# Expert rows and weights as scaled float16 pairs, the gathered rows transposed by DMA

## The reference

```python
def _sage_layer(h, src, dst, W_self, W_neigh, b, n_nodes):
    agg = segment_sum(h[src], dst, num_segments=n_nodes)
    deg = segment_sum(ones_like(dst), dst, num_segments=n_nodes)
    h_neigh = agg / maximum(deg, 1.0)[:, None]
    return relu(h @ W_self + h_neigh @ W_neigh + b)

x = x + sage(sage(layernorm(x)))
xf = layernorm(x)
topv, topi = top_k(xf @ Wg, 2); gate_w = softmax(topv)
h = relu(einsum('td,edh->teh', xf, W1) + b1)          # 8 experts, 512 x 512 each
y = layernorm(einsum('teh,ehd->ted', h, W2) + b2) * gamma + beta
x = x + sum(gate_w * y at topi)
```

## Time and profile before

| | |
|---|---|
| three runs | 2905.79, 2911.72 and 2912.53 us; median 2911.72 |
| the profiled execution | 2904.27 us, span 2902.5 us |
| mean granted TensorE clock | 0.95 |
| PE, DVE, ACT, POOL busy | 82%, 54%, 29%, 69% of the span |
| layer 1, layer 2, experts | about 140 to 1146, 1175 to 2165, 2192 to 2902 us |

### The profile page before, as it was taken

The page is one execution under the profiler, slowest core; times in us unless marked ns, Lnnn a source line. Parts: engine busy times, 40 slices in busy tenths (PEclk is TensorE's granted clock), DMA queues, the critical chain, the costliest instruction groups (busy, mean ns, idle before and its releaser), DMA issues.

```text
span 2902.5 us, 55359 instructions
## 1 busy us (share of the span) xinstructions
PE 2393.3 (82%) x11308; PEld 1537.2 (53%) x11309; DVE 1566.9 (54%) x3789; ACT 842.7 (29%) x1611; POOL 2004.7 (69%) x2229
## 2 busy tenths in 40 slices
PE   1088887878888777788888888898987999999996
PEld 0044444444444444455555555455556778888885
DVE  8665444545444444344445454444446677777775
ACT  6511211212211111111111111111114555555554
POOL 0277777777777775777777777777755666666665
PEclk9998989998989999899999999999998999999998
DMA  7578999899897776888888788888875765666543
GB/s 272 212 219 301 301 303 306 300 303 301 297 307 244 231 233 187 294 253 260 253 256 258 256 263 254 258 252 259 256 235 135 164 140 119 142 138 133 107 80 62
DMA packets 239323, 663.61 MB, mean 229 GB/s; under 512 B 47224, under 2 KB 48818, under 8 KB 236168
## 3 DMA queue, kind: packets, MB, share of 16 engines
q0 software_dynamic: 151472, 464.79, 55.8%
q10 hardware_dynamic: 62388, 128.09, 12.4%
q1 hardware_dynamic: 25380, 69.89, 7.5%
HBM read 550.93 MB, written 111.69 MB: 228 GB/s over the span
## 4 chain that ended last, share of the span: by engine, by line
POOL 46%; PE 21%; issue 16%; DMA 11%; DVE 2%; ACT 2%; SPq 1%; POOLq 0%; DVEq 0%; ACTq 0%
POOL store_all L728 45%; PE ps L1766 17%; DMA store_all<-h_scratch,srcT 5%; DMA store_all<-xn_scratch,srcT 2%; DMA wts<-expert_weights_scratch 1%; DMA out<-store_all,idx_s 1%; PE ps L1929 1%; PE ps L1941 1%; ACT store_all L857 1%; SPq L394 1%; ACT ln_out L857 1%; DMA xn_scratch<-store_all 0%; DVE ln_bst L1134 0%; PE ps L1796 0%; PE ps L1797 0%
## 5 line engine op out<-in xcount | busy, mean ns | idle before, releaser
L728 POOL DMA_INDIRECT store_all<-xn_scratch,srcT x782 | 776.3, 993 | 356.1 <-issue 230.1
L1796 PE MATMUL ps<-store_all,sel 128*128 x1680 | 682.2, 406 | 331.7 <-SPq L616 274.3
L728 POOL DMA_INDIRECT store_all<-h_scratch,srcT x782 | 760.2, 972 | 256.2 <-issue 224.3
L1797 PE MATMUL ps<-store_all,sel 128*128 x1680 | 671.4, 400 | 0.0
L1796 PEld LDWEIGHTS ps<-store_all,sel 128*128 128x128 f16 x1680 | 172.3, 103 | 698.6 <-issue 642.5
L1766 PE MATMUL ps<-wts,sT 128*128 128x512 f32 x1176 | 446.3, 492 | 0.0
L1766 PE MATMUL ps<-wts,aT 128*128 128x512 f32 x1176 | 400.7, 450 | 0.8 <-DVE aT L1375 0.8
L1337 DVE TENSOR_TENSOR sel<-iota_g,dstT 128x384 f16<-128x384 f32 (+2 forms) x602 | 306.4, 527 | 39.2 <-issue 30.2
L1766 PE MATMUL ps<-wts,m_hT 128*128 (+1 forms) x1224 | 312.9, 404 | 4.2 <-DVE m_hT L1642 4.2
L1766 PE MATMUL ps<-wts,m_xT 128*128 (+1 forms) x1224 | 311.4, 403 | 4.5 <-DVE m_xT L1585 3.6
L1766 PEld LDWEIGHTS ps<-wts,sT 128*128 128x128 f32 x1176 | 239.5, 211 | 93.4 <-issue 39.0
(11 more groups left out here) (299 smaller groups left out, 3063.5 us busy)
## 6 DMA issues: line engine op xcount, KB each, us to landing
expert_weights_scratch<-w_both ACTq DMA_DIRECT2D x64, 512.0 KB
wts<-expert_weights_scratch SPq DMA_DIRECT2D x64, 512.0 KB, 4.9
store_all<-in_L_ffn_W ACTq DMA_DIRECT2D x64, 256.0 KB, 5.5
of_experts<-xn_scratch ACTq DMA_DIRECT2D x49, 256.0 KB
of_experts<-h_scratch ACTq DMA_DIRECT2D x49, 256.0 KB
store_all<-in_x ACTq DMA_DIRECT2D x49, 256.0 KB, 4.8
store_all<-xn_scratch,srcT POOLq DMA_INDIRECT x782, 4.7
store_all<-h_scratch,srcT POOLq DMA_INDIRECT x782, 4.1
```

The lines of the kernel that those rows point to most:

```text
L728: pool.indirect_dma_start(rows[:, t % SLOTS, :], None, rows_d, bass.IndirectOffsetOnAxis(ap=srcT[:, t:t + 1], axis=0)).then_inc(s_rows[t % ...
L1796: pe.matmul(agg_p[p], sel[:, s, :], row[:, 0:D], start=k == 0, stop=False)
L1797: pe.matmul(agg_p[p], sel[:, s, :], row[:, D:2 * D], start=False, stop=False) \
```

## The change

- The experts' weights are multiplied by a power of two, found on the chip, and stored as pairs of float16. Layer 1 reads the weights twice, in 16 chunks of two row blocks: in tiles 4 to 19 DVE takes maximum and minimum of each chunk (`scan`); in tiles 20 to 22 the bounds go through HBM to all partitions and become scales; in tiles 24 to 39 the chunks are split.
- The normed rows are written as float16 pairs scaled by 2^11. Layer 2 has one activation and one subtraction more for it (`norm_lo`), and the store comes after the copy of xT.
- The weights of two experts now fill one half of `wts`, so expert 1 is loaded with expert 0 at the start of layer 2. An expert is four pieces of 512 KB, not eight.
- In the experts ACT issues one DMA transpose per tile, from the gathered pair of rows straight into the transposed operand; PE's four transposes of x, ACT's copy and DVE's subtraction are gone. The products are float16, three passes as before.

The diff, cut to its core:

```diff
+NCH = NB // 2
+SCAN0 = 4
+SPLIT0 = SCAN0 + NCH + 4
+assert SPLIT0 + NCH <= NT - 3
...
 
 
         wts_all = sb("wts", [P, 4, 2, KC, D], F32R)
         wts = [wts_all[:, 2 * i:2 * i + 2] for i in range(2)]
-        wts_e = wts_all[:].rearrange("p a h k n -> p (a h k n)").rearrange(
-            "p (r k h m n) -> p r k h m n", r=2, k=KC, h=2, m=2)
+        wts_e = wts_all[:, 0:2].rearrange("p r h k n -> p r (h k n)").bitcast(F16).rearrange(
+            "p r (c h m b n) -> p r c h m b n", c=2, h=2, m=2, b=2)
         store_all = sb("store_all", [P, 32, D])
         rows, w_raw = store_all[:, 0:SLOTS].bitcast(F16), store_all[:, 24:32].rearrange("p (m k) n -> p m k n", m=2)
-        raw_blocks = store_all[:, SLOTS:SLOTS + 2]
         bias_all = sb("bias", [2, 2, D], F32R)
...
+            loop0 = head
+            for g0, n, more in early:
+                for g in range(loop0, g0):
+                    tile(g, g % 2, between.get(g, {}))
+                pairs(g0, g0 + n, more)
+                loop0 = g0 + n
...
-                for k in range(KC):
+                for c in range(2):
                     for h in range(2):
-                        sp.dma_start(wts_e[:, par, k, h].bitcast(F32), wsplit_d[e * KC + k, :, h] if isinstance(e, int) else
-                                     wsplit_d[bass.ds(e * KC + k, 1), :, h].rearrange("a p m n -> (a p) m n")) \
+                        sp.dma_start(wts_e[:, par, c, h].rearrange("p m b n -> p m (b n)"),
+                                     wsplit_d[e * 2 + c, :, h] if isinstance(e, int) else
+                                     wsplit_d[bass.ds(e * 2 + c, 1), :, h].rearrange("a p m n -> (a p) m n")) \
                             .then_inc(s_expert[par], 16)
                         if landed is not None:
-                            alone(sp, s_expert[par], landed + 16 * (2 * k + h + 1))
+                            alone(sp, s_expert[par], landed + 16 * (2 * c + h + 1))
...
-                    sp.wait_ge(s_wst, 32 * NB + 1)
+                    sp.wait_ge(s_wst, SPLIT_DONE)
                     load_expert(0, 0)
+                    load_expert(1, 1)
...
-            sp.wait_ge(L[1]["dense"], NT)
-            load_expert(1, 1)
...
+            def gather_x(q, half, used=None):
+                if used is not None:
+                    alone(pool, M["xT"][half], used * 16)
...
+                gather_x(q + 3, 1 - half, pair + (1 + half))
...
                 def store_norm(n, p):
-                    alone(act, S["xn2"], n + 1)
+                    alone(act, S["xnlo"], n + 1)
                     if not (isinstance(n, int) and n == 0):
                         alone(act, S["xst"], n * 16)
                     for r in own_rows(n):
-                        act.dma_start(rows_at(xn2_d, n)[r], xn2_t[r]).then_inc(S["xst"], 16)
-
-                def load_raw(b, p):
-
-                    act.wait_ge(s_wset, 2)
-                    alone(act, s_wl, b + 1)
+                        act.dma_start(rows_at(xn2_d, n)[r], pair[r]).then_inc(S["xst"], 16)
+
+                def load_raw(c, p):
+
                     for m, w in enumerate((W1, W2)):
-                        act.dma_start(raw_blocks[:, m], w.rearrange("e (k p) n -> (e k) p n", p=P)[bass.ds(b, 1)]
-                                      .rearrange("a p n -> (a p) n")).then_inc(s_wraw, 16)
-
-                def store_split(b, p):
-                    alone(act, s_wl, b + 2)
-                    for h, t in enumerate((w_hi, w_lo)):
-                        act.dma_start(wsplit_d[bass.ds(b, 1), :, h].rearrange("a p m n -> (a p) m n"),
-                                      t.bitcast(F32)).then_inc(s_wst, 16)
+                        act.dma_start(raw_chunk[p][:, m].rearrange("p (b n) -> p b n", b=2),
+                                      w.rearrange("e (c b p) n -> (e c) p b n", b=2, p=P)[bass.ds(c, 1)]
+                                      .rearrange("a p b n -> (a p) b n")).then_inc(s_wraw, 16)
+
+                def load_scan(c, p):
+                    alone(act, s_scan, c + 1)
+                    load_raw(c, p)
+
+                def load_split(c, p):
+                    act.wait_ge(s_bound, SCANNED + 1)
+                    alone(act, s_wl, c + 1)
+                    load_raw(c, p)
+
+                def store_bounds(c, p):
+                    act.wait_ge(s_bound, SCANNED)
+                    act.dma_start(wmax_d[:, :], w_abs3[:]).then_inc(s_wmove, 16)
+
+                def load_bounds(c, p):
+                    act.wait_ge(s_wmove, 16)
+                    act.dma_start(of_experts[:, 3 * D:3 * D + 3 * P],
+                                  wmax_d.rearrange("(a p) c -> a (p c)", a=1).to_broadcast([P, P * 3])).then_inc(s_wmove, 16)
+
+                def store_split(c, p):
+                    alone(act, s_wl, c + 3)
+                    for h in range(2):
+                        act.dma_start(wsplit_d[bass.ds(c, 1), :, h].rearrange("a p m n -> (a p) m n"),
+                                      w_halves[:, h]).then_inc(s_wst, 16)
...
-                def expert_hi(b, p):
-
-                    alone(act, s_wraw, b * 32 + 32)
-                    act.wait_ge(s_wst, b * 32 + 1)
-                    act.activation(w_hi, raw_blocks, ACT.Copy).then_inc(s_wh, 1)
+                def expert_hi(c, p):
+
+                    alone(act, s_wraw, c * 32 + (NCH + 1) * 32)
+                    act.wait_ge(s_wst, c * 32 + 1)
+                    act.wait_ge(s_bound, SCALED_W)
+                    act.wait_ge(s_wset, 2)
+                    for m in range(2):
+                        i = act.activation(w_halves[:, 0, m], raw_chunk[p][:, m], ACT.Identity, scale=w_sc[:, m:m + 1])
+                    i.then_inc(s_wh, 1)
...
                 def norm2(n, p):
                     act.wait_ge(S["nmr"], n + 1)
                     act.wait_ge(S["xT"], n)
                     act.wait_ge(S["xst"], n * 16)
-                    act.activation(xn2_t, x2_t[:], ACT.Identity, bias=nmr[:, 0:1],
-                                   scale=rstd[:, 0:1]).then_inc(S["xn2"], 1)
+                    for to in (pair[:, 0:D], xn2_t):
+                        i = act.activation(to, x2_t[:], ACT.Identity, bias=nmr[:, 0:1], scale=rstd[:, 0:1])
+                    i.then_inc(S["xn2"], 1)
...
-                    hooks.update({4: [(sqrt2, 2)], 6: [(norm2, 2)], 8: [(store_norm, 2)], 10: [(xT_copy, 2)], 3: [(load_x, 1)]})
-                layer(act, l, hooks, early={4: [load_raw], 11: [expert_hi], 14: [store_split]} if l == 0 else None,
+                    hooks.update({4: [(sqrt2, 2)], 6: [(norm2, 2)], 10: [(xT_copy, 2), (store_norm, 2)], 3: [(load_x, 1)]})
+                layer(act, l, hooks, early=() if l else
+                      ((SCAN0, NCH, {4: [load_scan]}),
+                       (SPLIT0, NCH, {4: [load_split], 11: [expert_hi], 14: [store_split]})),
+                      between={SCAN0 + NCH: {12: [store_bounds]}, SCAN0 + NCH + 1: {12: [load_bounds]}},
                       drain=drain if l else None)
...
-            def x_hi(q):
-                act.wait_ge(M["xT"], q + 1)
-                act.wait_ge(M["h"], q)
-                act.activation(m_xT[:, 0].rearrange("p k n -> p (k n)"), mxT_p, ACT.Copy).then_inc(M["xHi"], 1)
+            def transpose_x(half, landed):
+                alone(act, M["x"][half], landed)
+                act.dma_start_transpose(m_xT[:, half], m_x2[:, half]).then_inc(M["xT"][half], 16)
...
-                    i = act.activation(m_hr[:, k, :], mhT_p[:, k * P:(k + 1) * P], ACT.Relu, bias=bias)
+                    i = act.activation(m_hr[:, k, :], mhT_p[:, k * P:(k + 1) * P], ACT.Relu, bias=bias,
+                                       scale=h_sc[:, 0:1])
...
+            transpose_x(0, 16)
+            transpose_x(1, 16)
+
+            def tile_m(q, half, pair):
...
-                x_hi(q + 1)
...
+                transpose_x(half, pair * 16 + 32)
...
+                def scan(c, p):
+
+                    alone(dve, s_wraw, c * 32 + 32)
+                    for t, op in ((scan_max, ALU.max), (scan_min, ALU.min)):
+                        i = dve.tensor_reduce(out=t[:, bass.ds(c, 1), :].rearrange("p a m -> p (a m)"), in_=raw_chunk[p],
+                                              axis=AX.X, op=op)
+                    i.then_inc(s_scan, 1)
+
+                def own_bounds(c, p):
+
+                    dve.wait_ge(s_scan, NCH + 2)
+                    dve.wait_ge(s_wg, 32)
...
+                def weight_scales(c, p):
+
+                    dve.wait_ge(s_wmove, 32)
+                    bstep(dve.tensor_reduce(out=w_bound[:], in_=w_every.rearrange("p q c -> p c q"), axis=AX.X, op=ALU.max))
...
+
+                def expert_lo(c, p):
+
+                    dve.wait_ge(s_wh, c + 1)
+                    for m in range(2):
+                        i = dve.scalar_tensor_tensor(out=w_halves[:, 1, m], in0=raw_chunk[p][:, m], scalar=w_sc[:, m:m + 1],
```

(57 more changed lines are left out.)

119 lines of the change are left out of this document (80 added, 39 removed).

## The result

The changed kernel takes 2975.28 us (median of 4 runs, 2962.66 to 2985.97) against 2909.02 for the kernel before on the same chip: a ratio of 1.0227 [1.0201, 1.0252]. It is slower, where 2857 us were forecast. The profiled execution is at the upper end of its runs (span 2984.2 us, 81.7 more than before's), so some 15 us of that difference are spread between runs.

A forecast was written before the change was run, and what follows sets the result against it. POOL's gather issue was taken to bound the graph layers and PE the expert stage. From the profiled 2904.3 us, minus 55 (expert tiles) plus 5 (layer 1), 1 (layer 2) and 2 (first tiles) gave 2857 us, range 2810 to 2970.

The forecast's parts named there:

- Layer 1: Tiles that scan or split weights: longer work on DVE and ACT, at most 48 us uncovered, taken as 5 us.
- the cover: Layer 1: PE's own slack, 93.1 us of waits for arrivals in 32 tiles, 2.9 us each, hides the added work.
- Layer 2: Extra activation and subtraction of 0.8 us a tile, covered by ACT's 5.6 us wait for PE; 1 us for the drain.
- The expert tile: Expert stage: period falls from 6.63 to 6.08 us, 0.55 saved in each of 100 tiles, 55 us.
- No idle gap stands on PE, so PE sets this pace: Expert stage before the change: PE's transposes and products fill the 6.63 us tile; 0.1 us off is 10 us off the kernel.
- The DMA transpose: Expert tile: 0.9 us issue on ACT with 2.16 free, 4.9 us landing with 7.7 free, so no cost.
- the scatter chain: Expert stage rival: scatters waiting on one another, 6.58 us apart beside the transpose's 256 KB; 2907 us, chance 0.11.
- Transposes that land late: Expert stage rival: at 8.8 us landing 2912 us, each 2 us more costing another 100; chance 0.05.
- the expert weights' loads: Expert stage: loads halve to four pieces per expert and delayed nothing with PE busy throughout; 0 us.
- The rival that forecast 2972: Expert stage, ACT queue: a transpose issue of 3.31 us makes ACT pace tiles at 7.23 us; chance 0.19.
- The rule that spoke against the change: Expert tile: transpose 128x128 on TensorE, 390 ns against 1309 by DMA; eight blocks 10.5 us, 7.5 us a tile, 2996 us.
- The first tiles: Start of the expert stage: first three tiles gain a transpose's latency in place of PE, ACT and DVE steps; 2 us.

The follow-up runs named there:

- h's chain short: Scale moved off the relu, high half of h first in the second product: changed kernel 2977.5 us; with float32 x transposed on TensorE 2883.7 us.

## Why the prediction was wrong

**Layer 1: right, and cheaper still.** Twelve profiled kernels share after's scan and split tiles: their layer 1 lasts 1007.9 to 1022.6 us, 1013.7 on average, against 1013.3 before. The 5 us forecast were nothing; the cover held, and the 6 us of the profiled execution are spread between runs.

**Layer 2: the wrong cover.** 1 us was forecast, 14 to 18 came. The step named ACT's wait for PE as what hides one more activation and one more subtraction. But its own first paragraph says that the layer lasts as long as POOL's gathers take to issue, and whether the subtraction slows those was not asked. It does, by 13.7 us / 49 = 0.28 us a tile. The Trainium skill has this in "GPSIMD Engine Reference", section Specifications: POOL's way to SBUF is shared with VectorE, and VectorE instructions with two SBUF inputs contend with it. The subtraction has two, and the trace agrees (1.96 against 0.95 us); that the shared way is the cause no run here shows by itself.

**The expert tile: the step that failed first** is "No idle gap stands on PE, so PE sets this pace". PE's ends are modelled. In the earlier trace rows the low half of h ends at 2506.52 and the second product starts at 2506.87: 0.35 us, the same as in after. So before's tile was 3.40 + 0.35 + 2.88 = 6.63 us, a chain of h already, and PE alone needed 6.46. The forecast took 0.04 for that hand-over "as between ACT and DVE there". With 0.35 its tile would have been 6.39. The second term is the relu: its new per-partition scale was in the diff, and was not costed; 1.50 us instead of 1.14. Then 3.69 + 0.35 + 2.59 = 6.63: the chain grew by as much as the product shrank. Of the 55 us nothing was left; that the tile is 6.63 us on both sides is a coincidence. The term for the product (2.64) was right: 2.59.

**The DMA transpose: the mechanism was mis-sized.** Its issue, taken as 0.9 us, is 1.26 and delayed no relu by much in 80 of 102 tiles, as argued, since 2.16 us were free. Its landing was taken as 4.9 us, and that is its median in after (by the landing semaphores, 104 transposes); but 11 take over the 7.7 us that were free, the longest 13.2. The rows of x, which ACT waits for, land in 4.6 us (median) to 13.2, and in 4.1 to 8.9 without transposes. The two transposes that stand alone land in 3.2 to 3.9. What was missing is that it isn't "another 256 KB": it takes 2.7 times the engine time of a plain copy of these bytes, and lifts the DMA share from 0.55 to 0.81. The sign of the scatter chain, rival at 0.11, came (101.8 us of waits for 28.3), though its sum added bytes and not packets; what it costs by itself no run shows. Transposes that land late came too, most of the latest beside weight loads: POOL's gathers waited 38 us for m_xT, the transposed x, and PE 21.6, half of that in the first tile; who waited for the transposes in after (us, times):

```profile
  POOL store_all L786: 38.0, 15
  PE ps L2037: 21.6, 5
```

The 0 taken for the expert weights' loads failed with them, as they meet: 22.6 us of the stage.

**The rival that forecast 2972** is near the result by accident: a transpose's issue does not take 3.31 us and ACT does not pace every tile. Its queue does hold the relu, in 22 tiles, and in the longest of these because the transpose waits for rows that come late.

**The rule that spoke against the change**, of the Trainium skill's "VectorE: DVE Perf Modes", sections The three transpose paths and Rules for kernel authors, was worked out to 2996 us, near too, and it holds here: with h's chain short, the version with TensorE transposes takes 2883.7 us and that with DMA transposes 2977.5. The estimate that led to 2996, eight blocks one behind another at the page's 1309 ns each, does not hold: eight land together in 3.2 to 3.9 us, and in 4.9 by the median beside the other traffic. So that this sum came near is luck.

**The first tiles**: 3 us were forecast (2 and the drain's 1). From the last gather to the second tile it was 48.8 + 8.26 us before, 51.6 + 13.69 after: 8 us. PE waits 10.59 us for the first transposed x, and the first relu stands behind the third transpose, which waits for its rows. No experiment takes these tiles apart. The first product of after:

```profile
2223.13 5.00 PE L2037 MATMUL ps<-wts,m_xT 128*128 128x512 f16 x12 [10.59 <-DMA m_xT<-store_all]
```

The sum, by the medians: 2857 + 55 (chain of h) + 44 (transposes, their meeting with the weights included) + 16 (layer 2's low halves, net of the 1 forecast) + 5 (first tiles) - 5 (layer 1) = 2972, against 2975. The forecast stood on a profiled execution 4.7 us below the median of before, so from that median it is 2977. The shares hold in this order alone: with the DMA transposes in place, a shorter chain of h gains nothing.

## What to carry to other kernels

Before calling an engine the bound, set the end of its input's producer beside its own start: where the same short distance (0.35 us here) stands in every tile, the chain through that hand-over may be the bound, however full the busy column looks, and a run that moves the wait tells. Cost a DMA by its packets and the engine time they take from every other queue, not by its bytes or its landing alone; and for a new vector instruction in a stage that lasts as long as another engine's issue, ask first what it does to that issue.

## What was not expected of the hardware

A product of twelve float16 matmuls takes 2.75 us, but 4.19 after PE had waited 3.1 us and 5.00 after 10.59 us. Windows of after over the first product of the stage, one in the stall above, and an undisturbed stretch (granted clock is the third number from the end):

```profile
2223.00:2228.00 5.00, 4.87 (x12) 1.66 (x12) 2.10 (x4) 0.00 (x0) 3.25 (x12) 0.53 0.92 87
...
2351.00:2355.30 4.30, 4.19 (x12) 1.44 (x12) 0.33 (x2) 0.65 (x2) 2.94 (x4) 0.65 0.90 188
2592.00:2595.00 3.00, 3.00 (x17) 1.39 (x15) 2.23 (x6) 2.29 (x6) 1.74 (x3) 1.00 0.45 78
```

At a mean of 0.53 the clock was at the lower of its two levels (1.2 GHz) for nearly all of that stretch, at 0.65 for most of the other, and at 1.00 it was at 2.4 GHz throughout. So a late transfer was paid for twice: 3.13 us of waiting and 1.44 us of slower matmuls at 2351.09.

A relu of 128x128 from PSUM takes 369 ns with a bias per partition (median of before; four are 1.14 us) and 457 ns with bias and scale per partition (median of after; four are 1.50).
